# Eight dense experts per token replaced by one: choosing in token order, scattering rows by expert, and 40 sorted tiles

## The reference

```python
xf = x.reshape(-1, 128)                                   # 4096 rows
H = gelu(xf @ W1 + b1)                                    # 4096 x 512
probs = softmax(H @ Wg + bg, axis=-1)                     # 8 experts
assign = argmax(probs, axis=-1)
for e in range(8):
    y = H @ Wd[e] + bd[e]                                 # 512 -> 128
    out = out + where(assign == e, probs[:, e:e+1] * y, 0.0)
```

## Time and the profile before

| | us |
|---|---|
| median of 3 runs (1526.89 to 1830.92) | 1527.73 |
| span of the profiled execution, first to last instruction | 1525.2 |
| its clock over the span | 0.972 of full |
| first attention, from 73 to 419 | 346 |
| recurrence with its start, from 419 to 879 | 460 |
| second attention, from 932 to 1295 | 363 |
| experts, from 1295.3 to 1525.2 | 229.9 |

### The profile page before, as it was taken

The page is one execution under the profiler, slowest core; times in us unless marked ns, Lnnn a source line. Parts: engine busy times, 40 slices in busy tenths (PEclk is TensorE's granted clock), DMA queues, the critical chain, the costliest instruction groups (busy, mean ns, idle before and its releaser), DMA issues. The chain is left out here.

```text
span 1525.2 us, 28287 instructions
## 1 busy us (share of the span) xinstructions
PE 1371.0 (90%) x8095; PEld 839.0 (55%) x8155; DVE 1327.9 (87%) x2378; ACT 1091.3 (72%) x1737; POOL 713.4 (47%) x950
## 2 busy tenths in 40 slices
PE   5599999999959999999999767999999996899998
PEld 4344444444428888888888753444444442455544
DVE  5789999999979999999999866899999997567665
ACT  6477777777739999999999655887887774434240
POOL 4144545455539999999999650223233332000000
PEclk9799999999989999999999988999999999899999
DMA  6055555555400000000000022555555550000000
GB/s 246 1 179 186 194 189 193 190 193 183 147 0 1 0 0 0 0 0 0 0 0 0 0 111 83 195 193 191 193 193 193 193 193 28 1 15 8 14 8 14
DMA packets 27312, 142.07 MB, mean 93 GB/s; under 512 B 2297, under 2 KB 10626, under 8 KB 10754
## 3 DMA queue, kind: packets, MB, share of 16 engines
q1 hardware_dynamic: 27266, 141.49, 26.3%
HBM read 139.39 MB, written 2.10 MB: 93 GB/s over the span
## 5 line engine op out<-in xcount | busy, mean ns | idle before, releaser
L882 PE MATMUL r_p_y<-w_ffn,r_z_t 128*128 128x128 f32 x1920 | 253.2, 275 | 26.5 <-ACT r_z_t L919 23.0
L882 PEld LDWEIGHTS r_p_y<-w_ffn,r_z_t 128*128 128x128 f32 x1920 | 253.4, 192 | 6.2
L992 POOL TENSOR_TENSOR r_stat<-r_stat,minus_half 128x4 f32<-128x4 f32 x240 | 242.0, 1008 | 18.8
L582 DVE SCALAR_TENSOR_TENSOR b_prob<-b_adj,b_prob 128x1024 f32<-128x1024 int32 x128 | 188.1, 1473 | 24.6 <-ACT b_prob L502 24.3
L538 POOL TENSOR_TENSOR b_lo<-b_prob,b_hi 128x1024 f16<-128x1024 f32 x32 | 79.9, 2498 | 257.2 <-ACT b_hi L509 257.2
L582 DVE SCALAR_TENSOR_TENSOR a_prob<-a_adj,a_prob 128x1024 f32<-128x1024 int32 x128 | 182.1, 1422 | 20.3 <-ACT a_prob L502 20.3
L502 ACT ACTIVATE b_prob<-b_p_s,shift,g_unit 128x1024 f32<-128x1024 f32 x128 | 154.0, 1203 | 52.3 <-PE b_p_s L438 52.1
L502 ACT ACTIVATE a_prob<-a_p_s 128x1024 f32<-128x1024 f32 x128 | 131.0, 1023 | 73.9 <-PE a_p_s L438 73.9
L951 DVE BATCH_NORM_STATS2 r_parts<-r_z 128x6 f32<-128x256 f32 x480 | 182.2, 422 | 1.3 <-ACT r_z L906 1.3
L944 DVE SCALAR_TENSOR_TENSOR r_h<-r_tanh,r_p_y 128x512 f32<-128x512 f32 x240 | 164.4, 685 | 4.1 <-ACT r_tanh L902 1.6
L538 POOL TENSOR_TENSOR a_lo<-a_prob,a_hi 128x1024 f16<-128x1024 f32 x32 | 81.6, 2551 | 181.1 <-ACT a_hi L509 181.1
(11 more groups left out here) (247 smaller groups left out, 3081.9 us busy)
## 6 DMA issues: line engine op xcount, KB each, us to landing
a_adj<-in_adj_t SPq DMA_DIRECT2D x64, 1024.0 KB, 4.8
b_adj<-in_adj_t SPq DMA_DIRECT2D x64, 1024.0 KB, 4.8
x_rows<-in_x SPq DMA_DIRECT2D x4, 512.0 KB, 7.2
wd_raw<-in_wd SPq DMA_DIRECT2D x1, 2048.0 KB
out_x<-e_acc SPq DMA_DIRECT2D x8, 256.0 KB, 2.3
late<-in_late SPq DMA_DIRECT2D x1, 756.0 KB
early<-in_early SPq DMA_DIRECT2D x1, 192.0 KB, 3.7
rows<-in_rows SPq DMA_DIRECT2D x1, 1.5 KB
```

The source lines that it names most:

```text
L582: nc.vector.scalar_tensor_tensor(prob[st][:], adj[transfer % ADJ][:, st % 2, :], 0.0, prob[st][:], ALU.is_gt, ALU.mult).then_inc(s["masked ...
L882: last = nc.tensor.matmul(out[:, D * t:D * t + D], z_t[g % R][:, P * t:P * t + P], k.w_ffn[:], start=False, stop=(t == TPC - 1), skip_grou ...
L992: nc.gpsimd.tensor_tensor(stat[g][:, 1, :], stat[g][:, 0, :], k.minus_half[:], ALU.pow)\
```

## The change

The block `experts` becomes two blocks, `choose_experts` and `run_experts`.

The first goes through the 8 chunks in token order. It makes H again with 12 products of 512 columns, but in f32, and computes the logits as 16 exact f32 products instead of 48 f16 ones. VectorE picks the expert and, with PE's help (`ranks`: 14 small bf16 products that count rows), finds for each row its place in its expert's region of a new tensor `sorted_rows` in device memory, 8 regions of 4096 rows. Each row is packed as 260 f32 numbers (normalised row, x, row number, gate), and GpSimd scatters the chunk with four indirect DMAs. There are two buffers `pack`; the rows of chunk c+2 are normalised only after the scatter of chunk c has landed. At the end `table` computes, for 40 tiles, which expert and which 128 rows of `sorted_rows` each one is.

The second works on 10 groups of four such tiles. SP reads each tile's row number into a register and loads the tile from `sorted_rows`. H is made a second time, ScalarE and VectorE cut it into halves. For each tile PE reads the expert's column from memory into a register and computes one expert: one f32 product for the bias and 12 f16 products of 128 columns. VectorE multiplies by the gate and adds x, and GpSimd scatters the four tiles to the output with four indirect DMAs; rows that hold nothing carry a row number that is out of bounds and are dropped.

Before that, `sorted_rows` has to be filled with blank rows: SP writes all of it, 32,896 rows of 1,040 bytes (34.2 MB), in 8 DMAs during the recurrence. In the diff the three loops `for c in range(CHUNKS)` of the first block stand in the order PE, ScalarE, VectorE; the indirect DMAs behind them are in GpSimd's loop; `both(q)` in the second stands for four gelus and four high halves of one group on ScalarE. Small tables are made by five `iota` on GpSimd in `normalise_a` and four VectorE instructions in `prepare_weights`, where three that cut the gate's weights are gone. The bias rows become one f32 row, and their tensor `bd` is cleared first.

```diff
-            for to, of in ((k.late[:], "late"), (k.rows[:], "rows"), (k.bd[0:E, :], "bd"), (k.wd[:], "wd")):
+            for to, of in ((k.late[:], io["late"]), (k.rows[:], io["rows"]), (k.wd[:], io["wd"])):
...
+            sp.wait_ge(preset, 1)
+            sp.dma_start(k.bd[0:1, :], io["bd"].rearrange("e d -> (e d)").unsqueeze(0)).then_inc(k.late_in, 16)
...
+            nc.vector.memset(k.bd[:], 0.0)
...
+            nc.gpsimd.iota(k.tags[:], [[P, T]], base=0, channel_multiplier=1, allow_small_or_imprecise_dtypes=True)
...
-            nc.vector.tensor_scalar(wg, wg, k.e_scale[:, 2:3], None, ALU.mult).then_inc(s["wg"], 1)
...
+            nc.vector.tensor_scalar(k.bd[:], k.bd[:], k.e_scale[:, 0:1], k.e_scale[:, 1:2], ALU.mult, ALU.mult)
...
+            for i in range(BLANKS):
+                last = each * (i + 1) + (1 if i == BLANKS - 1 else 0)
+                sp.dma_start(rows[:, each * i:last, :], k.blank[:].unsqueeze(1).broadcast_to([P, last - each * i, ROW]))\
+                    .then_inc(k.blanked, 16)
...
+def choose_experts(k, order, routed):
...
+            for c in range(CHUNKS):
+                if c + 1 < CHUNKS:
+                    turn_rows(c + 1)
+                logits(c)
+                if c + 1 < CHUNKS:
+                    hidden(c + 1)
+                ranks(c)
...
+            for c in range(CHUNKS):
+                if c + 1 < CHUNKS:
+                    front(c + 1)
+                    gelus(c + 1)
+                exps(c)
...
+            def rows(c):
+                if c > 1:
+                    dve.wait_ge(sent[c % 2], 16 * TPC * (c // 2))
+                    dve.wait_ge(s["ft_ready"], c - 1)
+                for t in range(TPC):
+                    last = normalised(k, pack[c % 2][:, t, 0:D], c, t)
+                last.then_inc(s["f_ready"], 1)
...
+            for c in range(CHUNKS):
+                if c + 1 < CHUNKS:
+                    rows_low(c + 1)
+                choose(c)
+                weigh(c)
+                places(c)
+                if c + 2 < CHUNKS:
+                    rows(c + 2)
+            table()
...
+                for t in range(TPC):
+                    nc.gpsimd.indirect_dma_start(k.sorted, bass.IndirectOffsetOnAxis(to_row[par][:, t:t + 1], 0),
+                                                 pack[par][:, t, :], None).then_inc(sent[par], 16)
...
+def run_experts(k, order, routed):
...
+                    row = sp.value_load(routed[0:1, j:j + 1], min_val=0, max_val=E * REGION)
+                    sp.dma_start(got[q % RING][:, t, :], k.sorted[ds(row, P), :]).then_inc(got_in[q % RING], 16)
...
+                own = ds(pe.value_load(order[0:1, j:j + 1], min_val=0, max_val=(E - 1) * D), D)
...
+                nc.tensor.matmul(out, k.ones[:], k.bd[:, own], start=True, stop=False)
...
+            for q in range(GROUPS):
+                if q + 1 < GROUPS:
+                    hidden(q + 1)
+                for t in range(TPC):
+                    product(q, t)
+                if q + 2 < GROUPS:
+                    turn_rows(q + 2)
...
+            for q in range(1, GROUPS):
+                both(q)
+                if q + 1 < GROUPS:
+                    front(q + 1)
...
+                    nc.gpsimd.indirect_dma_start(k.io["out"], bass.IndirectOffsetOnAxis(to_row[par][:, t:t + 1], 0),
+                                                 done[par][:, t, :], None, bounds_check=N - 1, oob_is_err=False)\
+                        .then_inc(stored[par], 16)
```

More of the change, by code:

```diff
@@ L1429, in product @@
-            def product(c, par, first, r):
-                t, half = r // 2, r % 2
-                if not (first and r < 2):
-                    pe.wait_ge(s["sum_step"], SUMS * (ROUNDS * c + r - 1))
-                rows = slice(P * t, P * t + P)
-                out = p_y[half][:].rearrange("p e d -> p (e d)")
-                for h in range(HC):
-                    w_hi, w_lo = (w[:, h, 4 * half:4 * half + 4, :].rearrange("p e d -> p (e d)")
-                                  for w in (k.wd_hi, k.wd_lo))
-                    nc.tensor.matmul(out, hid_hi[par][:, h, rows], w_hi, start=(h == 0), stop=False)
-                    nc.tensor.matmul(out, hid_hi[par][:, h, rows], w_lo, start=False, stop=False)
-                    last = nc.tensor.matmul(out, hid_lo[par][:, h, rows], w_hi, start=False, stop=(h == HC - 1))
-                last.then_inc(s["y_ready"], 1)
@@ L1443, in chunk @@
-            def chunk(c, par, first=False, last=False):
-                if not first:
-                    turn_gate(c, False)
-                if not last:
-                    turn_rows(c + 1, False)
-                for r in range(ROUNDS):
-                    product(c, par, first, r)
-                    if r == 0 and first:
-                        turn_gate(c, True)
-                    if r == 0:
-                        biases(c, first)
-                    if last:
-                        continue
-                    for h in HIDDEN[r]:
-                        hidden(c + 1, h, False)
-                    if r == LOGITS:
-                        logits(c + 1, 1 - par, False)
@@ L1461, in _, with ranks @@
-            turn_rows(0, True)
-            for h in range(HC):
-                hidden(0, h, True)
-            logits(0, 0, True)
-            chunk(0, 0, first=True)
-            chunk(1, 1)
-            with pe.Fori(1, CHUNKS // 2 - 1) as cc:
-                chunk(2 * cc, 0)
-                chunk(2 * cc + 1, 1)
-            chunk(CHUNKS - 2, 0)
-            chunk(CHUNKS - 1, 1, last=True)
+            def ranks(c):
+                pe.wait_ge(s["choices"], c + 1)
+                if c > 0:
+                    pe.wait_ge(s["taken"], c + 1)
+                hot = one_hot[c % 2]
+                for t in range(TPC + 1):
+                    if t < TPC:
+                        nc.tensor.matmul(p_rank[:, t, :], k.before_row[:], hot[:, t, :], start=True, stop=(t == 0))
+                    for u in range(t):
+                        last = nc.tensor.matmul(p_rank[:, t, :], k.ones_bf[:], hot[:, u, :], start=(t == TPC and u == 0),
+                                                stop=(u == t - 1))
+                last.then_inc(s["rank_ready"], 1)
@@ L1589, in step @@
-            def step(c, par, last=False, rows_left=True):
-                if not last:
-                    rows_low(c + 1)
-                begin(c, par)
-                for r in range(ROUNDS):
-                    add(c, par, r)
-                    if last:
-                        continue
-                    for h in HIDDEN[r]:
-                        lows(c + 1, 1 - par, h)
-                    if r == LOGITS - 1 and rows_left:
-                        rows(c + 2, False)
-                    if r == LOGITS:
-                        choose(c + 1)
-                    if r == LOGITS + 1:
-                        weigh(c + 1, 1 - par, False)
@@ L1607, in _ @@
             rows_low(0)
[L1608 removed]
             for h in range(HC):
[L1610 to L1619 removed]
+                lows(0, h)
+            rows_low(1)
@@ L1622, in build, with experts @@
+def experts(k):
+    with ExitStack() as span:
+        order, routed = (k.sb("x_" + n, [P, TILES], I32, span) for n in ("order", "routed"))
+        choose_experts(k, order, routed)
+        run_experts(k, order, routed)
 def build(nc, io):
```

478 lines of the change are left out of this document (304 added, 174 removed).

## The result

The changed kernel takes **1611.14 us** (median of 4 runs, 1607.49 to 1611.48) against 1527.6 us before. The ratio is 1.054, with a 95% interval of 1.0525 to 1.0557: 5.4% slower. The forecast was 1593 us, 4.3% slower, within 1545 to 1680. The profiled execution's span is 1609.1 us, its time 1610.9 (one of the four runs of before, at 1830.92 us, was a disturbed one; it is left out of the ratio).

A forecast was written before the change was run, and what follows sets the result against it. It took PE, with 165 us of wide products, to bound the experts' block. Passes of 187 + 107.5 = 294.5 against 229.9 us, and +1, make the span 1590.8, the median 1593 us (4.3% slower), range 1545 to 1680.

The forecast's parts named there:

- First pass: choose_experts over 8 chunks: 187 us (132 to 263), more than PE's whole 165 us of wide products.
- round trips: First pass, from one scatter's landing to the next: 24.75 us (17.2 to 35), coming six times, 148.5 us.
- Second pass: run_experts over 10 groups, from the first loads to the last scatter: 107.5 us (94 to 154).
- the start: Second pass, first loads through H to the low halves and the next group's cast and low half: 20 us.
- The step: Second pass, one group to the next, set by PE's own loop: 8.5 us (7.8 to 12.7), 8 times.
- The end: Second pass after the last H: low halves 7, product 4, finish 1.6, scatter 6.9 us.
- ScalarE's loop: Second pass, H, four gelus and high halves, next group's cast and low half: 7.8 us per group.
- Around it: Outside the experts: weights' preparation +1 us (+0.6 to +1.7); clearing, iota and filling of sorted_rows hidden.
- Full clock: Rival for both passes: full clock and a quick scatter give 132 + 94 = 226, 1525 us, no change; chance 0.13.
- Dear descriptors: Rival on GpSimd's scatters in both passes: 2.55 us per scatter and 4.8 to land, 1675 us; chance 0.17.
- The register loads stall PE: Rival in the second pass: 12.7 us per group, +38 us, 1631 us; chance 0.10.
- The scatter costs nothing: Rival in the first pass: scatter lands as fast as VectorE reaches the next rows, 1497 us, 2% faster; chance 0.05.

The follow-up runs named there:

- the run with the rows ahead: Changed kernel with four row buffers, and VectorE normalising the rows of chunk c+2 ahead of the choice of chunk c: 1523.16 us.
- all that helped: Changed kernel with four row buffers, rows normalised before the choice, five gathered-tile buffers, transposes before each group's last tile: 1507.14 us, ratio 0.987.

## Why the prediction was right, and where it was off

**The verdict and its cause** were right: PE's 165 us of wide products went, and the first pass is a round trip that costs more than they did. The two passes came out differently: the first as predicted, partly by luck, the second 19 us longer.

**First pass: 187 us predicted, 187 measured** (1295 to 1482). By the terms: to the first landing 31.2 against 32.7; then five round trips of 24.5 us in the mean (1326.54 to 1449.23) against 24.75; the rest 32.8 against 30.25. That the trip fits within 0.2 us is luck to about 1 us. In the trip shown, the longest, logits and H took 6.7 and 5.1 us. Over the six, H took 3.9 to 5.1, so that the two together were 11.1 in the mean, where I had taken 10.5 between 6.2 and 12.4. VectorE's wait for the scatter was 7.25 in the mean instead of 6.9; in the trip shown it is 7.35, of which the issue is 4.8 (I had 4.6 from GpSimd's 1.15 us) and the landing with the row numbers' hand-over to GpSimd 2.6 (2.3). These 0.95 us too little are made up by `weigh`, `places` and their hand-overs, 1.6 us instead of 2.45, and by the transposes, 0.9 instead of 1.1. That the scatter is on the path is shown by the run with four buffers, that the logits are by the run with these first. The Trainium skill, *DMA: Bandwidth & Descriptors*, section Anatomy of one DMA, puts most of some 2 us per DMA into the receipt of the write and calls the making of descriptors small. The 1.8 us from the last issue's end fit; that the issue is small does not: one takes 0.97 us, and the four in a row are two thirds of the wait. So the trace disagrees on the issue, and the low end near which this put a scatter was not reached.

**Second pass: 107.5 us predicted, 127 measured.** This is the term that was mis-sized, and almost all of the 18 us between forecast and result. Split as in the prediction: the start 17.9 us against 20 (1482 to H of the second group, 1499.94); eight steps 82.7 against 68; the end 26.5 against 19.5.
- *The step, 10.3 against 8.5* (11.8 for the first, in which H still runs at half clock, 5.1 us instead of 2.6; 10.1 for the others). "PE's sequencer can read ahead while the array works, so I count none of it in the loop" failed in part. The narrow products are cheaper than my 0.067 us:

```profile
1524.18 0.22 PE L1665 MATMUL e_p_y<-wd_hi,e_hid_hi 128*128 x1
1524.24 0.22 PE L1666 MATMUL e_p_y<-wd_lo,e_hid_hi 128*128 x1
```

  0.055 us apart, the low end of the estimate, so a group's tiles are 4 x (0.22 + 12 x 0.055) = 3.5 us of work; they take 4.64 in the run with five buffers, 1.1 us more, most of it ahead of the fourth tile, which starts 1.7 to 1.9 us after the third. The Trainium skill's 81 ns for such a pair of load and product (*TensorE: Matmul & The Clock Gate*, section Back-to-back issue gap) is not borne out by these rows. Transposes cost 0.65 instead of 0.45. That gives 9.3 with H and the wait for the low half, which are as predicted. That SP's 6.0 per group "fit" failed as well: it compared a rate, where the ring makes a loop of `finish`, four loads in a row, their landing, transposes, low half, H and product. It is worth some 0.5 us per group by the run with five buffers.
- *The end, 26.5 against 19.5.* The last product took 6.6 us (1590.76 to 1597.33) instead of 4, and a wait of 0.8 ahead of it; its tiles start 1.78 us apart where their work is 0.88. Of these 0.9 us some 0.65 stand ahead of the bias product, where the register load is, and the rest inside the tile, where register arithmetic (`REGISTER_ALU`) stands between the products. That it is the register instructions, which nothing hides any more, fits these places, but no run tested it. The last scatter took 10.5 us from the end of `finish` at 1598.56, issue 5.6 and 4.9 to the span's end, where I had 6.9 with the short landing of 2.3; the range's other end of 4.8 was the right one for a transfer that nothing follows.
- Once rows and order no longer cover it, groups come 7.7 us apart, close to the 7.8 that the prediction worked out for ScalarE's loop. But PE is by then busy for 37.2 of 38 us (1430 to 1468), so which of the two closes the loop isn't shown.

**Around it: +1 us predicted, 0 measured.** The clearing of `bd` costs 0.91 us and falls into the wait for x, the dearest `iota` costs 0.26 in GpSimd's gap, and the experts' first instructions stand where they stood:

```profile
1.07 0.91 DVE L221 MEMSET bd_rows<- 128x1024 f32 x1 [0.18 <-issue]
...
9.26 0.26 POOL L300 IOTA before_row<- 128x128 bf16 x1
...
1295.30 0.61 POOL L1590 COPY c_pack<-x_rows 128x512 f32<-128x512 f32 x1 [0.50 <-SPq L1357]
```

The +1 of the weights' preparation is not to be seen at the experts' start. The filling of `sorted_rows` is hidden, and faster than I counted: slices 12 and 13 of the page show 336 and 335 GB/s, so 34 MB take about 100 us and not 300, long before the recurrence ends. The issues with size and landing:

```profile
sorted_rows<-blank SPq DMA_DIRECT2D x7, 4160.0 KB, 32.7
...
sorted_rows<-c_pack,c_to_row POOLq DMA_INDIRECT x32, 2.5
```

**Rivals.** Full clock did not come (0.57). The rival's reason, "the logits keep PE's rows dense after each wait", does not hold: in the run with the rows ahead the rows are dense (busy for 19.9 of 20 us), and the clock is 0.68. "Dear descriptors" fell with 0.96 us per indirect DMA (its bad end for the scatter is 15.0 us by its own terms, 4 x 2.55 + 4.8, and not 15.2, which changes nothing). "The register loads stall PE" is there, if these waits are theirs, to a quarter of its price (1.1 of 4.2 us per group) in the steady state, and nearly in full in the last product. "The scatter costs nothing" did not hold with two buffers, where VectorE waits 7.25 us for it in each trip; with four it does.

## What to carry to other kernels

A stage that became a loop through several engines and a transfer is sized by adding its parts in series, not by the busiest engine; and the remedies to try first are more buffers and an earlier place in an engine's order. Here they turned 5.4% slower into 1.3% faster with no work removed. Not every move pays, though: the exponentials first gave half of what was expected, since the ranks stood behind H too, and H mixed into the logits cost 15 us. When two waits take turns on one engine, mend both before judging either. Where a queue "fits" by its rate, also follow what it waits for round to itself.

## What was not expected of the hardware

- The granted clock fell while PE was busy for 99% of the time: 0.68 with f32 logits of 8 columns, 1.00 with f16 logits and wide products in the same time. The Trainium skill, *TensorE: Matmul & The Clock Gate*, section What's actually happening, says that the clock follows how busy PE has been; these two rows show equal busy time at different clocks, so busy time as the profile counts it does not tell the clock. Logits and fillers were changed together between them.
- The order of the same work moved it too: 0.50 to 0.59 with H cut up between logits, against 0.62 to 0.76 with H in one piece (all that helped). In the windows at 0.59 PE also idled for 1.5 to 1.8 of 20 us.
- After fillers at full clock, 2 idle us still showed 1.00, and the logits after 3.5 us of gap 0.50.
- An indirect DMA of 128 rows costs GpSimd 0.96 to 0.98 us and 0.30 of gap, now and then up to 1.43 in place of the 0.98.
